# Attention with relative positions and a mixture of experts: routed experts computed only for their own rows, through slot tiles in DRAM

## What is computed

```
x = x + _L0_attn_ref(_layernorm(x), ...)
xt = _layernorm(x).reshape(-1, 128)
scores = softmax(xt @ gate_w.T)
_, idx = top_k(scores + gate_bias, 2)
weights = take_along_axis(scores, idx, axis=1)
y = 0
for e in range(8):
    gate_e = sum(where(idx == e, weights, 0.0), axis=1)
    h = silu(xt @ w1[e].T) * (xt @ w3[e].T)
    y = y + gate_e[:, None] * (h @ w2[e].T)
z = silu(xt @ sw1.T) * (xt @ sw3.T) @ sw2.T
x = x + y + z
```

## Time and profile before

| | |
|---|---|
| median of 3 runs | 774.75 us (773.13 to 775.63) |
| profiled execution, first to last instruction (span) | 770.0 us |
| what lies around the span (median less span) | 4.75 us |
| PE busy | 690.5 us, 90% |
| DVE busy | 589.2 us, 77% |
| ACT busy | 514.7 us, 67% |
| POOL busy | 255.8 us, 33% |
| DMA | 138.48 MB, mean 180 GB/s |

### The profile page before, as it was taken

How to read it: one execution, slowest core, us unless ns; L and a number is a source line. 1 busy time by engine, 2 the same in 40 slices (tenths; PEclk the granted TensorE clock), 3 DMA queues, 4 the chain that set the end, 5 groups by cost and what they waited for, 6 DMA issues and landing times. The chain is left out here.

```text
span 770.0 us, 27094 instructions
## 1 busy us (share of the span) xinstructions
PE 690.5 (90%) x10316; PEld 507.9 (66%) x10368; DVE 589.2 (77%) x2036; ACT 514.7 (67%) x1032; POOL 255.8 (33%) x253
## 2 busy tenths in 40 slices
PE   4687879899888899988999988988999999999997
PEld 3465657677666677766777766766666666666665
DVE  7965686788787788787888887977566776677676
ACT  3686967688797878888888998887335343443331
POOL 9443445334355534545543445533000000000000
PEclk9988989999999999999999999999999999999999
DMA  9899998689989778787778779841000000000000
GB/s 255 262 295 335 333 303 264 203 244 277 309 250 302 255 222 253 249 238 241 236 222 266 221 232 255 271 153 50 3 22 28 29 5 23 28 15 1 14 15 14
DMA packets 117839, 138.48 MB, mean 180 GB/s; under 512 B 8976, under 2 KB 86288, under 8 KB 117520
## 3 DMA queue, kind: packets, MB, share of 16 engines
q1 hardware_dynamic: 117712, 136.75, 58.6%
HBM read 82.26 MB, written 54.46 MB: 178 GB/s over the span
## 5 line engine op out<-in xcount | busy, mean ns | idle before, releaser
L1075 DVE CUSTOM_DVE_ANT_0 ps<-ps,near 128x128 f32<-128x128 f32 (+3 forms) x512 | 245.1, 509 | 90.5 <-PE ps L837 57.0
L998 ACT ACTIVATE work<-ps,nmin 128x128 f32<-128x128 f32 (+3 forms) x512 | 248.4, 548 | 54.2 <-DVE nmin L1075 49.4
L849 PE MATMUL ps<-ident,work 128*128 128x128 f32 x1280 | 202.6, 278 | 20.7 <-issue 11.6
L849 PEld LDWEIGHTS ps<-ident,work 128*128 128x128 f32 x1280 | 157.0, 143 | 36.5 <-issue 13.7
L795 POOL TENSOR_SCALAR_AFFINE_SELECT work<-work 128x512 f32<-128x512 f32 x96 | 61.5, 641 | 237.8 <-ACT work L987 203.6
L1392 ACT ACTIVATE near<-ps 128x512 f32<-128x512 f32 x80 | 47.5, 595 | 133.3 <-PE ps L1357 133.2
L799 POOL TENSOR_TENSOR work<-work 128x512 f32<-128x512 f32 x96 | 124.2, 1294 | 8.0
L1060 DVE COPY work<-ps 128x512 f32<-128x512 f32 (+1 forms) x192 | 123.2, 642 | 2.5 <-issue 1.6
L837 PE MATMUL ps<-kb,qb 128*128 128x384 bf16 (+3 forms) x460 | 110.6, 298 | 12.3 <-ACT work L998 9.4
L1367 PEld LDWEIGHTS ps<-work,near 128*128 128x128 f32 x640 | 82.6, 192 | 34.2 <-issue 31.6
L987 ACT ACTIVATE work<-ps 128x512 f32<-128x512 f32 (+1 forms) x160 | 90.2, 564 | 18.7 <-PE ps L849 18.1
(11 more groups left out here) (111 smaller groups left out, 627.3 us busy)
## 6 DMA issues: line engine op xcount, KB each, us to landing
near<-w_slots SPq DMA_DIRECT2D x96, 512.0 KB, 5.4
w_slots<-relS SPq DMA_DIRECT2D x128, 256.0 KB, 4.5
qk_rows<-work SPq DMA_DIRECT2D x36, 256.0 KB, 4.7
near<-w_slots SPq DMA_DIRECT2D x32, 256.0 KB, 4.6
qk_rows<-y SPq DMA_DIRECT2D x9, 256.0 KB, 6.8
qb<-qk_rows SPq DMA_DIRECT2D x24, 96.0 KB
kb<-qk_rows SPq DMA_DIRECT2D x24, 96.0 KB
qb<-qk_rows SPq DMA_DIRECT2D x48, 48.0 KB
```

Of the source, the lines that this page charges most:

```text
L849: ins = nc.tensor.transpose(tp_ps[:, m % 2, n * P:(n + 1) * P], prob[:, m % PROBS, n * P:(n + 1) * P], ident[:, :])
L998: ins = nc.scalar.activation(prob[:, m % PROBS, h * wide:(h + 1) * wide], qk_ps[:, m % 3, h * wide:(h + 1) * wide], ACT.Exp, bias=nmin[:, ...
L1075: nc.vector.tensor_tensor_reduce(out=scores, in0=scores, in1=near[:, q % NEAR, a, 4 * P - wide:4 * P, r], scale=1.0, scalar=3e38, op0=ALU. ...
```

## The change

The 4096 rows are taken as 4 batches of 8 tiles (`BATCHES`, `BT`). For each batch the routing is turned into places: every row is sent to two slots, one for each expert that it uses; the slots of one expert stand together, padded to whole tiles of 128. The padded number of tiles is at most 23 (`RT`), and 23 tiles are always computed, in 6 rounds of 4 tiles (the last has 3): 24 rounds in all.

- DVE works out the places: `gates_count`, `gates_place`, `gates_map` take the place of `gates_write`. PE helps with two small matmuls a batch (`prefix`).
- POOL scatters the normalised rows to `xs_dram`, one indirect DMA for each tile and choice: 64 DMAs of 128 rows of 512 bytes. Later it gathers the results from `ys_dram` with another 64.
- Before that, SP clears the slots with 24 DMAs (`clear_slots`), put into the last slots of the attention.
- A round: SP loads the slots (`load_slots`), PE turns them (`turn_slots`), DVE copies them (`copy_slots`), ACT copies the weights of the four tiles' experts into a buffer (`copy_weights`: a load of expert numbers into registers, then four copies of 128x384), PE forms eight matmuls 128x128, ACT the silu, DVE the product with the second result, PE four matmuls 128x128, ACT copies the result (`take_product`), SP stores it (`store_slots`).
- The order of steps is a list: the two shared blocks of chunks 0 to 4 (steps 0 to 9), the 24 rounds (10 to 33), the shared blocks of chunks 5 to 7 (34 to 39).
- DVE adds the gathered rows, scaled by the two weights, two tiles at a time (`combine`, 16 lots): lots 0 to 3 at steps 28 to 31, lots 4 to 7 at steps 35 to 38, lots 8 to 15 behind the last step. There are 4 buffers for gathered lots (`YGS`), so the gather of a lot waits for the combine of the fourth before it.
- The chunks of `x1` all have a place of their own now, and SP stores the output only from combined chunks.

```
+BATCHES = 4
+BT = TILES // BATCHES
+RT = (TOPK * BT * P + E * (P - 1)) // P
+ROUND = 4
+ROUNDS = -(-RT // ROUND)
+NR = BATCHES * ROUNDS
+CLEARS = NR
+FRONT = 5
+SEQ = ([("shared", c, m) for c in range(FRONT) for m in range(NSH)] + [("round", r, 0) for r in range(NR)]
+       + [("shared", c, m) for c in range(FRONT, CHUNKS) for m in range(NSH)])
+TURN_AT = [-1, 0, 1, 2, 3, 4, ROUND_AT + 1, ROUND_AT + 2]
+PREFIX_AT = [5, 7, 9, ROUND_AT + 7]
+COMBINE_AT = [*range(28, 32), *range(35, 39)]
...
+                    if 0 <= m - FIRST[NQ - QUADS] - 2 < CLEARS:
+                        experts["clear"](sp, m - FIRST[NQ - QUADS] - 2)
...
     def pool_program(pool):
-        for e in range(E):
-            ins = nc.gpsimd.memset(order[:, e:e + 1], float(E - e))
-        ins.then_inc(order_done, 1)
+        pool.wait_ge(zero_out, 16 * CLEARS)
+        for g in range(BATCHES):
+            pool.wait_ge(pos_done, g + 1)
+            pool.wait_ge(xn_done, BT // CT * (g + 1))
+            for n in range(BT):
+                for r in range(TOPK):
+                    c, m = divmod(g * BT + n, CT)
+                    nc.gpsimd.indirect_dma_start(
+                        xs_dram[g], bass.IndirectOffsetOnAxis(pos[:, g, r, n:n + 1], 0), xn[:, c, m, :], None,
+                        bounds_check=RT * P - 1, oob_is_err=False).then_inc(xs_out[g], 16)
+        for g in range(BATCHES):
+            for k in range(YOS):
+                pool.wait_ge(yo_out[k], 16 * len(range(k, ROUNDS * (g + 1), YOS)))
+            for n in range(BT):
+                lot = (g * BT + n) // 2
+                if n % 2 == 0:
+                    wait(pool, comb_done, TOPK * 2 * (lot - YGS + 1))
+                for r in range(TOPK):
+                    nc.gpsimd.indirect_dma_start(
+                        yg[:, lot % YGS, n % 2, r, :], None, ys_dram[g],
+                        bass.IndirectOffsetOnAxis(pos[:, g, r, n:n + 1], 0),
+                        bounds_check=RT * P - 1, oob_is_err=False).then_inc(yg_in[lot % YGS], 16)
...
     def sync_program(sp, wait_stored):
+        for j in range(CHUNKS - 2, CHUNKS):
+            wait_stored(sp, j)
+            load_tokens(sp, j)
+        for r in range(XGS):
+            load_slots(sp, r)
+        for r in range(NR):
+            store_slots(sp, r)
+            if r + XGS < NR:
+                load_slots(sp, r + XGS)
         for c in range(CHUNKS):
...
+            sp.wait_ge(comb_done, TOPK * CT * (c + 1))
+            sp.dma_start(out_tiles[:, CT * c:CT * (c + 1), :], x1c[c]).then_inc(out_done, 16)
...
+            pe.wait_ge(xgT_done, n + 1)
+            pe.wait_ge(wbuf_done, n + 1)
+            for k, (bank, ready) in enumerate(((h1_ps, h1_ready), (h3_ps, h3_ready))):
+                for a in range(tiles_of(n)):
+                    at = slice(a * P, (a + 1) * P)
+                    ins = nc.tensor.matmul(bank[s % 2][:, at], wbuf[:, n % WSETS, a, k * P:(k + 1) * P], xgT[:, n % 2, at],
+                                           start=True, stop=True)
+                ins.then_inc(ready, 1)
...
+        for s in range(NS + 2):
+            if s < NS:
+                hidden(s)
+            last_row(s)
+            if s + 1 < NS and SEQ[s + 1][0] == "round":
+                turn_slots(pe, SEQ[s + 1][1])
+            if s - 2 in PRODUCTS:
+                product(s - 2)
...
+        def copy_weights(r):
+            g, n = divmod(r, ROUNDS)
+            if n == 0:
+                act.wait_ge(emap_done, g + 1)
+            at = slice(ROUND * n, ROUND * n + tiles_of(r))
+            _, which = nc.values_load_multi_w_load_instructions(
+                emap[0:1, g, at], engines=[mybir.EngineType.Activation], min_val=0, max_val=E - 1,
+                skip_runtime_bounds_check_because="a count of seven comparisons")
+            if r >= WSETS:
+                act.wait_ge(y_ready, made(ROUND_AT + r - WSETS))
+            for a in range(tiles_of(r)):
+                ins = nc.scalar.activation(wbuf[:, r % WSETS, a, :], wr_v[:, bass.ds(which[a] * W, W)], ACT.Copy)
+            ins.then_inc(wbuf_done, 1)
```

More of the change, by code:

```diff
@@ L46 @@
 PROBS = 5
-WEIGHTS = 5
+WEIGHTS = 8
 MINS = 32
@@ L1195, in expert_part @@
     acc_done = sem("acc_done")
-    out_done = [sem(f"out_done2{n}") for n in range(2)]
+    yo_done = sem("yo_done")
+    yo_out = [sem(f"yo_out{n}") for n in range(YOS)]
+    yg_in = [sem(f"yg_in{n}") for n in range(YGS)]
+    comb_done = sem("comb_done")
+    out_done = sem("out_done2")
     x1_tiles = x1_dram.rearrange("b (i p) c -> p (b i) c", p=P)
     out_tiles = out.rearrange("b (i p) c -> p (b i) c", p=P)
-    LATE = 4
     SPLIT = [slice(0, TILES - GB * NI), slice(TILES - GB * NI, TILES)]
-    def additions(k):
-        return AC * (k // NY) + 1 + CT * (k % NY) if k >= 0 else 0
@@ L1207, in prepared_at, with tiles_of @@
-    def prepared_at(j):
-        late = LATE if j == 1 else 0
-        base = NM * (j - 1) + late
-        return {"normalise": base - late + 1, "turn": base + 2, "copy": base + 3, "scores": base + 4, "shift": base + 5,
-                "exp": base + 6, "softmax": base + 7, "pick0": base + (8 if j > 1 else 7),
-                "pick1": base + (9 if j > 1 else 8)}
-    def due(step, what):
-        return [j for j in range(1, CHUNKS) if prepared_at(j)[what] == step]
+    def tiles_of(r):
+        return min(ROUND, RT - ROUND * (r % ROUNDS))
@@ L1306, in then, with chained @@
+    rows = lambda v: v.unsqueeze(1).to_broadcast([P, BT, E])
+    def chained(dve, g, first):
+        step = [first]
         def then(ins):
             step[0] += 1
[L1308 to L1318 removed]
@@ new lines, in gates_map @@
+    def gates_map(dve, g):
+        v, then = routes[g % 2], chained(dve, g, 26)
+        wide7 = [P, RT, E - 1]
+        then(nc.vector.tensor_tensor(v["eq"], starts.unsqueeze(2).to_broadcast(wide7),
+                                     v["last"][:, 0:E - 1].unsqueeze(1).to_broadcast(wide7), ALU.is_ge))
+        with nc.allow_low_precision(reason="numbers of experts are whole"):
+            nc.vector.tensor_reduce(emap[:, g, 0:RT], v["eq"], AX.X, ALU.add).then_inc(emap_done, 1)
+        for r in range(TOPK):
+            then(nc.vector.tensor_tensor(v["tmp"][:, :, :], v["pick"][:, r, :, :], v["score"][:, :, :], ALU.mult))
+            then(nc.vector.tensor_reduce(wsel[:, g, r, :], v["tmp"][:, :, :], AX.X, ALU.add))
@@ L1382, in tensor_program @@
                     turn_tiles(pe, j)
-                for j in due(step, "scores"):
-                    gate_scores(pe, j)
-        product(CHUNKS - 1, NY - 1)
     def scalar_program(act, last_row):
-        exponentials(act, 0)
-        for k in range(NM * CHUNKS):
-            act.wait_ge(h1_ready, k + 1)
-            wait(act, hT_done, k - 1)
-            nc.scalar.activation(silu[:, k % 2, :], h1_ps[k % 2], ACT.Silu).then_inc(silu_done, 1)
-            last_row(k)
-            if k == NM * (CHUNKS - 4):
-                roots(act, 1)
-            for j in due(k, "normalise"):
-                normalise(act, j)
-            for j in due(k, "copy"):
-                copy_turned(act, j)
-            for j in due(k, "exp"):
-                exponentials(act, j)
```

548 lines of the change are left out of this document (350 added, 198 removed).

## The result

The change makes the kernel slower: **838.34 us** (median of 4 runs, 834.78 to 840.91) against 773.94 us for the kernel before (also 4 runs). The ratio is **1.084, with a 95% interval from 1.078 to 1.090**. The prediction said 747 us, in a range of 712 to 803. Later jobs showed that this verdict does not hold everywhere: the same program, in another job, took 764.28 us beside 769.62 us for the kernel before (one run of each).

The account below looks back on a forecast made before the run. POOL's queue of 128 indirect DMAs was taken as the bound: first DMA at 568.3 us + 165.6 queue + 6.1 end + 2 hops and waits = 742.0 us span; with 4.75 us to the median, 747 us, range 712 to 803.

Parts of the forecast that it names:

- The other work then fits under it: Expert part: PE's and ACT's rounds hide under POOL's 165.6 us of DMAs, with 15 us of slack at lot 8's gathers.
- a dearer t: Rival on POOL's queue: each indirect DMA costs over 1.51 us; 811 us at 1.8, 875 at 2.3; chance 0.22.
- dearer rounds: ACT's register loads and addresses at 3.4 us a round: rounds of 6.3 us, time 798 us; chance of slower 0.05.
- Price of an indirect DMA: POOL's queue: t = 1.29 us each, between 0.36 and 2.3, taken from POOL's 128x512 tensor op; 128 make 165.6 us.
- the slower reading of the Trainium skill: POOL's queue pays each indirect DMA's fixed part, 2.15 us each, 857 us instead of 747; SP's row speaks against it.
- First DMA: POOL's first scatter at 568.3 us: part starts at 540.1, PE's steps take 25.6 us, DVE's places 2.6 us.
- the clears: SP's 24 clears in the attention, 6.0 MB in some 34 us: costed at nothing, at most 3 us.
- POOL's queue solid: Sign of being right: POOL issues DMAs from 568 to 734 us, 1.29 us apart, but for small waits.
- The rounds: Expert part: 3.4 us a round, set by ACT, against 3.2 us on PE; 23 full rounds' worth take 78 us.
- The end: After POOL's queue: landing, additions and store 6.1 us, plus 2 us for hops and buffer waits.
- ACT as the bound: Rival: registers and addresses cost ACT 2 us a round, rounds take 4.9 us, time 765 us; chance 0.13.
- Cheap descriptors: Rival on POOL's queue: t = 1.0 us gives 714 us, t = 0.5 gives 693 us with PE alone; chance 0.13.

Follow-up runs that it names:

- jobs 1, 4, 5 and 7: Changed kernel as it is, 838.34, 842.89 and 837.18 us in the first three; in the last, only its first 32 indirect DMAs dense, the rest spaced, 823.0 us.
- job 6: Unmodified changed kernel, 764.28 us; with a waited-for memset behind each indirect DMA, 827.09; kernel before plus 128 dense dummy scatters, 776.93; kernel before alone, 769.62.
- job 1: The changed kernel against the kernel before, the result's own runs: 838.34 us against 773.94 us, ratio 1.084.
- the kernel with plain transfers: Changed kernel with its 128 indirect DMAs replaced by 24 plain ones of the same bytes, rows not sent to their experts: 723.41 us.
- the self-controlled kernel: Changed kernel with its first 32 indirect DMAs dense and a waited-for 128x1 memset behind each of the other 96: 823.0 us, ratio 1.061.
- the table's kernel: Changed kernel with the row numbers of every indirect DMA from a loaded table instead of computed places: 764.93 us in job 3, 841.59 us in another job.
- Job 2: Changed kernel with 24 plain DMAs, 723.41 us; with 128x256 memset pauses, 853.26. Kernel before with 128 dense dummy scatters, 772.99; with 96 spaced ones, 775.54.
- job 7: Changed kernel with its first 32 indirect DMAs dense and the other 96 spaced by a waited-for 128x1 memset: 823.0 us, ratio 1.061.
- job 3: Changed kernel variants: plain transfers plus 128 dummy scatters, 761.98 us; row numbers from a table, 764.93; plain gathers, 736.00; 128x1 memset pauses, 829.31.
- the burst: Kernel before with 128 indirect scatters of a constant tile to unread DRAM, back to back on POOL: 772.99 us, and 776.93 us in job 6.
- the spaced kernel: Changed kernel with a waited-for memset of 128x256 on POOL behind each indirect DMA, pitch 2.07 us: 853.26 us.

## Why the prediction was wrong

**The step that failed is the paragraph on POOL's queue where it says "The other work then fits under it".** It took for granted that other engines run at their own pace beside POOL's DMAs. Neither the sum nor any rival had a term for the opposite, so the range ended at 803 us, and the chance of slower rested on a dearer t (0.22) and on dearer rounds (0.05). In jobs 1, 4, 5 and 7 the engines are held up in dense bursts, and since DVE makes the places and combines that POOL waits for, POOL's chain, the bound, stretches. Compared with the undisturbed execution (span 762.5 us), the disturbed one (839.2) lasts 76.7 us longer. POOL's waits account for nearly all of it. Beyond the usual 0.30 us between two DMAs they are 83.6 us there and 7.0 us in the undisturbed one; less 4.0 us because the first DMA came earlier (576.9 against 580.9), that makes 72.6. Most of the other 4 us is the one slow gather at 806.99 (2.2 us more, behind 1.5 us of extra idle time). Why the engines are held up, and why only in some jobs, stays open.

The other steps are judged by the undisturbed execution of the same program in job 6.

*Price of an indirect DMA: right.* Predicted t = 1.29 us. Timeline of POOL in its last lot, and the groups of both lines:

```profile
749.48 1.00 POOL L1361 DMA_INDIRECT work<-ys_dram,near  x1 [0.30 <-issue]
750.78 1.00 POOL L1361 DMA_INDIRECT work<-ys_dram,near  x1 [0.30 <-issue]
752.09 1.00 POOL L1361 DMA_INDIRECT work<-ys_dram,near  x1 [0.30 <-issue]
...
L1361 POOL DMA_INDIRECT work<-ys_dram,near x64 | 64.0, 1000 | 19.5 <-issue 17.7 <-DVE relS L1672 1.5 <-DVE vb L1672 0.3
L1350 POOL DMA_INDIRECT xs_dram<-near x64 | 62.5, 976 | 58.4 <-DVE near L1520 39.5 <-issue 18.9
```

1.28 us for a scatter (0.97 and 0.30 between two) and 1.30 for a gather. The POOL operation of the earlier trace rows was a lucky neighbour, not a reason. A scatter lands 2.2 us after its issue (median) and the queue goes on after 1.28, so the slower reading of the Trainium skill (DMA: Bandwidth & Descriptors, Anatomy of one DMA), an estimate of 2.15 us each in the queue, is not what this trace shows; its word that most of the fixed part is completion latency fits.

*First DMA: 12.6 us late (568.3 predicted, 580.88).* 7.5 us of it is the start of the second part, 547.6 us instead of 540.1; in 16 executions of kernels with the new arrangement it lay between 539.5 and 551.8, so much of that varies from run to run. In four with the old arrangement it lay between 540.1 and 545.3, so a share of the clears, which the sum put at nothing, is not excluded. 2.9 us are PE's steps, 28.5 us instead of 25.6, mostly two waits that the count left out:

```profile
563.58 0.63 PE L933 MATMUL ps<-ident,y 128*128 128x128 f32 x4 [1.67 <-DVE work L1132]
...
573.34 0.68 PE L948 MATMUL ps<-wp,work 128*128 128x128 f32 x4 [1.13 <-ACT work L1053]
```

The last 2.1 us are the places: 4.7 us from PE's prefix to POOL instead of 2.6, since DVE had a sum of 0.66 us ahead of them and POOL started 0.9 us after the last step.

*POOL's queue solid: nearly.* It waited once, 7.32 us up to 649.43, for the places of the fourth batch, which are made only in the rounds (the prefix of that batch stands in step 17). The sum had no such term. Behind it come 79 DMAs with no wait over 0.4 us.

*The rounds: right in pitch.* Timeline of PE (the changed kernel, job 6): 3.44 us from one to the next once they run evenly, predicted 3.4.

```profile
691.22 2.02 PE L1552 MATMUL ps<-kb,qb 128*128 128x128 f32 x16
...
694.66 2.02 PE L1552 MATMUL ps<-kb,qb 128*128 128x128 f32 x16
```

ACT's four addressed copies take 1.75 us together, as one row of the trace. The first hidden matmuls of a round came at 610.07 and the last at 697.87, 88 us instead of 78; 6.9 us of it are waits for DVE's copies of turned slots (L1647) and 1.6 us waits for ACT's silu. POOL's gathers never waited over 0.31 us for a combine, so this stayed hidden. PE's wait ahead of the first slots' turns was 11.7 us, not 20, since PE was itself late.

*The end: 9.1 us from the end of POOL's queue (752.09 + 1.30) to the end of the span, instead of 8.1.* And what lies around the span was 1.8 us in that execution; the 4.75 us of the prediction were mostly the distance of one execution to a median.

So the sum for an undisturbed job, put right: 580.9 + 128 x 1.29 + 7.0 + 9.1 = 762.1, against 762.5 of span. The gain predicted as 28 us came out as 5, within the spread of the kernel before; most of the rest went into POOL's later start (12.6 us), its one wait (7.0 us) and the end (1.0 us).

*The rivals.* Dearer descriptors: no, t stood as forecast. ACT as the bound: no. Cheap descriptors: no. POOL did wait for `comb_done` for long in job 1, which was listed as a sign of rounds as the bound; there the rounds were not slow by themselves but held up.

## What to carry to other kernels

An indirect DMA of 128 rows of 512 bytes costs POOL's queue about 1.3 us, so 128 of them are a serial stretch of some 165 us: count that, the place where the first can start, and every wait in it, and set it against the work saved (here 49 us by the kernel with plain transfers). Dense indirect DMAs can hold up the other engines in one job and not in the next, so measure such a kernel in more than one before you believe either a gain or a loss. When two kernels of an experiment ran in different jobs, the unchanged kernel beside them is not control enough (its medians were 770 to 779 us everywhere): send the disturbed kernel along.

## What the runs showed of the hardware

- **Hold-ups by job.** The changed kernel, or a variant with the same dense DMAs, was held up in four jobs (838.3, 842.9, 837.2 us; the self-controlled kernel's dense part) and not in two (764.3 us; the table's kernel 764.9 us against 841.6). Within a job all kernels with dense indirect DMAs of the new arrangement agreed. Job 2 had no such kernel; by its records (third point) it was of the undisturbed sort.
- **How they look.** They begin 6 to 14 us into a burst at a pitch of 1.28 us, starts of instructions come mostly 0.70 us or 1.40 us apart on DVE, and the long ones clear some 4 us after the burst (617.8 to 622.05, 717.1 to 721.24); in the longest burst some work got through in between, from 707.7 to 713.9. In the two long stretches the DMA engines have a share of 0.30 and 0.25. At a pitch of 1.86 us there were none in job 7; the pitch of 2.07 us ran in job 2 only and says nothing.
- **Semaphore records go missing with them.** Each indirect DMA raises its semaphore by 16, and in an undisturbed trace that is 16 events: 2038 of 2048 in job 6, 2026 to 2043 in job 3. In the held-up traces of kernels with 128 dense ones only 370 to 544 of 2048 are there. They are missing from the first 16 DMAs on (43 of 256 in job 1), whose first comes 15 us ahead of the first late step of DVE; and in job 7 they are still missing (94 of 256 for the second 16 spaced ones) where no engine is held up any more. All traces of job 2 are full: the burst has 2044 of 2048, the spaced kernel 2028. So its runs, like the burst of job 6, say nothing on what a dense burst does in a job with hold-ups.
- **What stays open.** Why it happens. In the held-up traces the indirect DMAs have no time from issue to landing, where the changed kernel's have 2.2 us otherwise, and waits name the releaser "remote", perhaps for want of those records. A rival that no run tests is that the recording itself, or the path that semaphore events share with it, takes part: every time in this document is of an execution that has a recorded span, and none is known to have run without. Other work on the chip during a job is another such rival. Whether a burst alone, beside the old arrangement, is enough was tried only in the undisturbed jobs 2 and 6. Pauses that are rarer than one for each DMA were not tried, nor a version with fewer indirect DMAs.
- **The clock follows.** A round of 12 matmul halves takes PE 1.57 us at the granted clock of 1.00, the level of 2.4 GHz (job 6, at 677.85). Behind the second long hold-up, at 708.55, it took 2.90 us, and from 708.0 to 711.5 the granted clock was 0.50, the level of 1.2 GHz: such a hold-up costs PE again when it resumes. A wait of another kind does the same: in job 6 a round of 16 took 3.14 us at 615.65, behind 3.11 us of waiting, against 2.02 us.
